# A four-layer graph network on one core: the order of its preparation, of its edge products and of the unread products on TensorE

## What is computed

```
x = layernorm(x + L0(x, adj))   # A_hat @ x, Linear(128, 256), batch norm, relu, Linear(256, 128), batch norm
x = layernorm(x + L1(x, adj))   # U^T @ x, Linear, relu, Linear, U @ out
x = layernorm(x + L2(x, adj))   # 4 attention heads over the 256 edges, softmax by source node
x = layernorm(x + L3(x, adj))   # two graph convolutions, then LSTMs of 1 to 4 steps over the nodes

# L1: the eigenvectors of the normalised Laplacian
deg = A.sum(0) + A.sum(1) - diag(A)
L_norm = deg**-.5 * (diag(deg) - A) * deg**-.5
_, U = eigh(L_norm)                         # 128 x 128, eigh reads the symmetric part
```

## Time and profile before

| | |
|---|---|
| three executions | 1038.46, 1037.54 and 1037.67 us, median 1037.67 |
| the profiled execution | 1037.68 us |
| its span | 1035.9 us, mean granted clock 0.921 |
| PE | 928.0 us busy (90%) |
| PEld | 606.9 us (59%) |
| DVE | 615.2 us (59%) |
| ACT | 603.3 us (58%) |
| POOL | 159.2 us (15%) |

### The profile page before, as it was taken

The page is one execution under the profiler, slowest core; times in us unless marked ns, Lnnn a source line. Parts: engine busy times, 40 slices in busy tenths (PEclk is TensorE's granted clock), DMA queues, the critical chain, the costliest instruction groups (busy, mean ns, idle before and its releaser), DMA issues.

```text
span 1035.9 us, 13392 instructions
## 1 busy us (share of the span) xinstructions
PE 928.0 (90%) x3987; PEld 606.9 (59%) x3987; DVE 615.2 (59%) x2155; ACT 603.3 (58%) x1520; POOL 159.2 (15%) x458
## 2 busy tenths in 40 slices
PE   3799867878888986999999999999999999999994
PEld 2555554455556664666888777885444466654442
DVE  5577766745668784477445797434544444544676
ACT  0456646736537773277644355535966688875556
POOL 0233333313333332000000000000000000000055
PEclk9799977867779896799999999999999999999998
DMA  9100000000000000000000000000000000000014
GB/s 257 49 1 1 0 1 1 1 1 1 1 1 2 1 1 1 1 1 1 1 1 1 1 2 1 1 1 0 1 1 0 1 0 1 1 0 1 0 41 122
DMA packets 14328, 12.99 MB, mean 13 GB/s; under 512 B 896, under 2 KB 11056, under 8 KB 14256
## 3 DMA queue, kind: packets, MB, share of 16 engines
q1 hardware_dynamic: 14018, 11.98, 4.1%
q10 hardware_dynamic: 238, 0.16, 0.1%
HBM read 7.89 MB, written 4.19 MB: 12 GB/s over the span
## 4 chain that ended last, share of the span: by engine, by line
PE 73%; DVE 16%; ACT 6%; issue 3%; DMA 1%; POOL 1%; ACTq 0%; DVEq 0%; POOLq 0%
PE bank L938 17%; PE bank L962 9%; PE bank L857 3%; PE bank L799 3%; PE bank L789 3%; PE bank L813 3%; PE bank L847 3%; PE bank L620 2%; PE bank L619 2%; PE bank L506 2%; PE bank L753 2%; PE bank L764 2%; PE bank L925 1%; PE bank L865 1%; PE bank L917 1%
## 5 line engine op out<-in xcount | busy, mean ns | idle before, releaser
L1409 ACT ACTIVATE hid_t<-bank,gate_b 128x512 f32<-128x512 f32 (+1 forms) x252 | 148.9, 630 | 48.9 <-PE bank L962 48.2
L1518 POOL TENSOR_SCALAR x<-x,perm 128x128 f32<-128x128 f32 x32 | 29.3, 928 | 592.7 <-DVE perm L2169 592.7
L962 PE MATMUL bank<-ms,w_t 128*128 128x512 f32 (+1 forms) x288 | 110.8, 528 | 0.1
L938 PE MATMUL bank<-hid_t,w_t 128*128 128x336 f32 (+1 forms) x296 | 106.6, 506 | 1.2 <-DVE x L2144 1.2
L938 PE MATMUL bank<-feat_t,w_t 128*128 128x512 f32 x208 | 93.1, 603 | 0.0
L938 PEld LDWEIGHTS bank<-hid_t,w_t 128*128 128x128 f32 x296 | 55.8, 190 | 46.2 <-issue 25.8
L962 PEld LDWEIGHTS bank<-ms,w_t 128*128 128x128 f32 x288 | 54.1, 190 | 48.1 <-issue 33.8
L938 PEld LDWEIGHTS bank<-feat_t,w_t 128*128 128x128 f32 x208 | 39.1, 189 | 51.0 <-issue 46.7
L1197 ACT ACTIVATE con<-bank,con 128x1 f32<-128x1 f32 x62 | 16.2, 261 | 89.3 <-PE bank L620 89.2
L1416 ACT ACTIVATE hid_t<-hid_t 128x512 f32<-128x512 f32 (+1 forms) x72 | 41.8, 581 | 34.9 <-DVE hid_t L2128 25.6
L1043 ACT ACTIVATE x<-x,perm 128x128 f32<-128x128 f32 x128 | 52.3, 482 | 2.6 <-DVE perm L1550 2.6
(11 more groups left out here) (420 smaller groups left out, 2121.7 us busy)
## 6 DMA issues: line engine op xcount, KB each, us to landing
out<-x SPq DMA_DIRECT2D x16, 256.0 KB, 3.0
con<-in_constants SPq DMA_DIRECT2D x1, 449.0 KB, 3.1
feat_t<-in_L_gnn_W SPq DMA_DIRECT2D x2, 128.0 KB, 3.6
e_int<-in_L_gnn_src ACTq DMA_DIRECT2D x1, 128.0 KB
l_w<-in_L_gnn_W SPq DMA_DIRECT2D x2, 64.0 KB
wg<-in_L_gnn_Wg SPq DMA_DIRECT2D x2, 64.0 KB
adj_n<-in_adj SPq DMA_DIRECT2D x1, 64.0 KB, 3.3
x<-in_x SPq DMA_DIRECT2D x4, 0.5 KB, 10.3
```

What stands on the lines that cost most here:

```text
L938: return mm(bank[4 * u + BANK_OF[g]][:, 0:w], w_t[:, WB_IH + 4 * (it.p - 1) + g, :], lstm_x(n), start=True, stop=(it.k == 0))
L962: mm(bank[4 * u + BANK_OF[g]][:, 0:w], w_t[:, WB_HH + 4 * (it.p - 1) + g, :], lstm_h_of(it.chain)[:, 0:w], start=False, stop=True).then_in ...
L1409: f(dst[:, 0:w], bank[4 * u + BANK_OF[g]][:, 0:w], ACT.Tanh if g == G_G else ACT.Sigmoid, bias=gate_b[:, 4 * (it.p - 1) + g:4 * (it.p - 1) ...
```

## The change

**Preparation.** DVE converts the edge numbers first, PE turns them and the first group of weights early. ACT makes the one-hot rows in place of DVE: 1 - |i - s| cut at zero by an Abs and a Relu of 128 columns for each half of the edges (`edge_columns`), the rank by a Sign of 256 columns that adds up its own row, then again Abs and Relu of 256 columns (`edge_places`). DVE keeps the key, two conversions and a doubled iota. DVE's `eigen_setup` follows right behind the Laplacian; `ahat_t`, the row sums and the columns of `v_rows` come behind it (`graph_columns`). The memsets stand at the start.

**Turn 0.** The edge products are spread over it: sources ahead of the first `pe_rows`, targets behind w, ends behind the diagonals, rows beside step 1, adjacency and starts behind step 1's rank update. DVE copies two of them (`edges_sorted`) behind its first next vector, ACT four (`edges_kept`, `edges_spread`) behind the row copy of step 2. The rest of DVE's edge work (`edge_rest`) stands at the start of layer 1.

**Layer 0.** All its constants are one slot higher. The first quarter of `x` has a semaphore of its own, on which the first aggregate waits; the fifth waits for the rest.

**Unread products.** `kept_busy` by slots is gone. In each turn but 0 and 8 stand two of 384 columns (`filled`): behind step 1's rank update, and ahead of the transposition. `without_products(slot)` is true for slots with no layer 0 work on PE (23, 40 to 44, 61 to 63), where `beside` adds 384 and 128 columns. Two of 384 stand ahead of `pe_kept_turned(HALF)` and one of 128 behind it.

**Order in a turn.** On PE, `beside(h2)` with layer 0's work stands ahead of the transposition, not behind it. DVE's next vector of step 1 stands ahead of the tangents, and ACT's part of it ahead of the row norm.

**Buffers.** `pair`, `pv_ident`, `kept` and `square` are new tiles of their own, in place of parts of `con`, `src_st`, `src_1h` and `dst_s`; the tangents use `con_f` and `con_b` in place of `perm`; the unread tiles `ys` go.

The core of the diff:

```diff
-QUIET, FULL_FROM = (41, 42, 43, 60, 61, 62), 36
-A_AGG, A_COPY, A_HID0, A_HID1, A_SAVE0, A_SAVE1, A_STATS = 0, 1, 1, 2, 2, 2, 4
-BN_ONE, B_RELU, B_OUT, B_KEEP, B_STATS = 20, 22, 23, 24, 25
+A_AGG, A_COPY, A_HID0, A_HID1, A_SAVE0, A_SAVE1, A_STATS = 1, 2, 2, 3, 3, 3, 5
+BN_ONE, B_RELU, B_OUT, B_KEEP, B_STATS = 21, 23, 24, 25, 26
...
             def beside(slot):            # PE
...
+                if without_products(slot):
+                    filled(384, slot == HALF - 1)
+                    filled(128, slot == HALF - 1)
...
+            def filled(cols, rows_read):
+                into = bank[5] if rows_read else bank[6]
+                mm(into[:, P:P + cols], ident, con[:, 0:cols], start=True, stop=True)
...
             def jacobi_turn(i):          # PE
...
-                pe_rows(h0)
-                kept_busy(h0)
-                pe_w(i)
-                beside(h0)
...
+                if i == 0:
+                    first_products(h0)
+                else:
+                    pe_rows(h0)
+                    pe_w(i)
+                    beside(h0)
...
                 behind_rank(h0)
                 pe_rows(h1)
-                kept_busy(h1)
+                if i == 0:
+                    edges_rows()
                 beside(h1)
                 pe_rank(h1)
                 behind_rank(h1)
+                if i == 0:
+                    edges_adjacent()
+                    edges_starts()
+                else:
+                    filled(384, True)
                 pe_rows(h2)
-                kept_busy(h2)
+                beside(h2)
+                filled(384, False)
                 pe_turn(i)
-                beside(h2)
                 pe_rank(h2)
...
+                filled(384, False)
+                filled(384, False)
                 pe_kept_turned(HALF, 1)
+                filled(128, False)
...
             def edge_places():           # ACT, new
+                for c in range(EC):
+                    link.mark(f(perm[:, c, :], sum_st[:, :], ACT.Sign, bias=rank[:, 0, c:c + 1], accum_out=rank[:, 1, c:c + 1]))
+                link.settle()
+                act.wait_ge(s["edge_cols"], 5)
+                for c in range(EC):
+                    link.mark(f(away[c][:, :], iota2, ACT.Abs, bias=rank[:, 1, c:c + 1]))
+                link.settle()
+                for c in range(EC):
+                    t = f(perm[:, c, :], away[c][:, :], ACT.Relu, scale=-0.5, bias=ones[:, 0:1])
+                t.then_inc(s["edge_hot"], 1)
...
             def jacobi_turn(i):          # ACT
...
                     act_matrix(h1)
-                act_row_norm(i)
                 if h1 is not None:
                     act_vector(h1 + 1)
+                act_row_norm(i)
                 behind_step(h1)
...
             def jacobi_turn(i):          # DVE
...
                 dve_reflected(h1)
+                dve_next(h1)
                 dve_tangents(i)
-                dve_next(h1)
```

269 lines of the change are left out of this document (150 added, 119 removed).

## The result

The changed kernel takes 999.26 us (median of 998.09 to 999.61), the kernel before 1038.07. The ratio is 0.9623 (95% interval 0.9607 to 0.9640): 38.8 us less. Run once more among the experiments it took 998.35 us (ratio 0.9617, 0.9601 to 0.9633). The forecast was 1009.0, in a range of 1000 to 1021. So the sign was right, the gain was 10 us larger than forecast, and the time lies 0.7 us under the range.

What follows compares the result with a forecast made beforehand. In the turns a chain of small steps over four engines was taken as the bound, if PE is on time. 1037.68 - 15.5 (preparation) - 2.0 (turn 0) - 12.0 (turns 1 to 15) + 0.8 (behind) gave 1009.0 us, range 1000 to 1021.

Steps and rivals of the forecast that it cites:

- turns 1 to 15: Unread products fill PE's gaps and hold the clock up: items of 15.1 us, taken as 12.0 less (5 to 18).
- the next vector ahead of the tangents: Second step of each turn: vector earlier but tangents as much later, taken as 0, 4 us either way in all.
- behind the turns: Ahead of the solve: two unread products before the turning of the kept columns delay PE, 0.8 us more.
- The preparation: Until DVE's first reflected row: it starts at about 15.4 instead of 30.90, 15.5 us less (13.5 to 16.5).
- Turn 0: First reflected row to turn 1: 22.3 us instead of 24.35, 2.0 less (5 less to 2 more).
- Turns 1 to 4: 22.4 us three times and 21.6, with 0.6 lost per turn to layer 0 ahead of the transposition: 0.8 less.
- Turn 5: ScalarE's 4.07 us wait for the batch norm's moments stays; 0.5 us less.
- The discount of 3.1: Turns 1 to 15: 12.0 us taken instead of 15.1, as some turns' new products and surrounding work would miss.
- That all gaps are filled: Rival: all gaps filled, also in the solve, with 3 us more in turn 0: 1001 us, chance 0.12.
- The start did not stall: Rival that the start stalls on ScalarE's one-hot chain and the late first kept column: 1013 us, chance 0.10.
- The slower rival: At 1.2 GHz, unread and layer 0 products cost some 3 us per turn on the chain: 1063 us, chance 0.02.
- the signs named: Reflected row at 15 to 16 us, turn 1 from 37 to 38, clock near 1.00 in turns 6, 7, 9 to 14.

Runs made afterwards that it cites:

- changed again: The changed kernel itself run once more, nothing altered, as the base for the runs beside it: 998.35 us, ratio 0.9617.
- before + new unread products: The kernel before with only the new unread products in the turns, its own ones gone, order and preparation as before: 1018.41 us, ratio 0.9809.
- the transposition ahead: The changed kernel with the transposition ahead of layer 0's products and the unread one in each turn's third step: 1024.20 us, ratio 0.9860.

## Why the prediction was right or wrong

The mechanism was right: the products in PE's gaps hold the clock up, and the start moves by what was forecast. Two terms of the sum were mis-sized. The 12.0 us for turns 1 to 15 measured 17.5 and 19.9 in the two traces, and the next vector ahead of the tangents, put at 0, is worth 3 to 4 of them. A third, behind the turns, had the wrong sign in the traces.

**The preparation: right.** L1770's successor (L1838) came at 15.59 us, forecast 15.4; 15.3 us less, forecast 15.5. The first edge product came at 12.01, forecast 12.4. ScalarE's operation of 256 columns took 0.51 us and not the 0.40 of the sum, which was read from a copy of that size, but the chain was early enough all the same. By the Trainium skill (ScalarE: Activation LUTs, What ACT_TABLE_LOAD costs) the estimate was 0.49, and the trace agrees with it.

**Turn 0: right, in part by luck.** From the first reflected row to turn 1 it was 22.4 us (15.59 to 37.99), forecast 22.3; in the second trace it was 20.6. The forecast had the clock up before step 1; it was in the second trace, and in the first it was down again (last section).

**Turns 1 to 4: the sum right, by two misses that cancel.** 0.7 us less, forecast 0.8. Turns 1 to 3 took 22.1 to 22.3 us each, forecast 22.4; turn 4 took 22.2, forecast 21.6, as the clock fell in it. Layer 0 ahead of the transposition costs 0.45, 0.46 and 0.26 us in turns 1 to 3 (forecast 0.6), by the kernel with layer 0 behind it at the same clock. Turn 5: 0.3 to 0.7 less, forecast 0.5. Its wait stands, and turn 11's too; ScalarE in turn 11 of the changed kernel:

```profile
265.01 0.20 ACT L1150 ACTIVATE sc<-sc 128x1 f32<-128x1 f32 x1 [4.38 <-DVE sc L1725]
```

**Turns 1 to 15: the sign right, the size the step that failed.** The items added up to 15.1 us, and 12.0 was taken, for turns in which the clock would fall all the same. Item by item:

| us less | forecast | changed | changed again | before + new unread products |
|---|---|---|---|---|
| turns 1 to 4 | 0.8 | 0.7 | 0.7 | 4.0 |
| turn 5 | 0.5 | 0.3 | 0.7 | 2.0 |
| turns 6 and 7 (to its last row product) | 2.4 | 3.8 | 3.8 | 2.4 |
| rest of 7, removal turn | 0 | -0.5 | -0.9 | -0.4 |
| turn 9 | 3.4 | 5.1 | 3.8 | 4.3 |
| turn 10 | 2.3 | 3.7 | 3.7 | 2.5 |
| turn 11 | 1.0 | 0.5 | 2.7 | 2.0 |
| turns 12 to 15 | 4.7 | 4.0 | 5.3 | 0.8 |
| together | 15.1 | 17.5 | 19.9 | 17.6 |

The discount of 3.1 was wrong: the clock still fell in turns 5, 8, 11 and 12 to 15, but turns 11 to 15 missed their items by no more than 1.2 us in one trace and passed them by 2.3 in the other, and in turns 6, 7, 9 and 10 it held nearly everywhere and they passed theirs. The items of turns 6, 7 and 10 were right for the unread products alone; what the changed kernel has above them there is the order. That the sum for turns 12 to 15 came near in the changed kernel and not with the products alone was not foreseen.

**The next vector ahead of the tangents: the step that failed by its mechanism.** It was taken at 0, because the tangents would come as much later. They do come later, but the transposition waits behind layer 0's and the unread product anyway, so nobody is late. It is worth 3 to 4 us by the run that undoes it, 0.6 in each of the turns 6 and 10 and 0.1 in turns 1 to 3. This lies inside the bounds of 4 us that the prediction gave, and the value between them was the wrong one.

**Behind the turns: the sign wrong in the traces, the size not told from nothing.** Forecast was 0.8 more. The traces show the solve 0.9 and 1.7 us shorter, with a part of it at full clock. What was to cost 0.8 cost about 0.2 by two traces: without the products PE waits 1.02 us for the kept column's load at that place, and the two fill it (from the start of turn 15's last product to the turning it is 1.41 us without them and 1.61 with them). Leaving the three out made no measurable difference in the median.

**Layers 1 to 3.** The 2.4 us less of the first trace belong to the clock at the start of layer 1, and the second trace has none of it.

**The sum.** The forecast was 28.7 us less (1037.68 - 1008.98). The spans of the two traces are 38.1 and 40.2 less, so 9.4 and 11.5 were missing. Of these, 5.5 and 7.9 are in turns 1 to 15 (3.1 for the discount, the rest about what the tangents' order brings), 1.7 and 2.5 behind the turns, 2.4 and -0.1 in layers 1 to 3, -0.3 and 1.9 in turn 0, and 0.1 and -0.7 ahead of the first row product. The last three move with the clock's chance and the start from trace to trace.

**The rivals.** That all gaps are filled (0.12, 1001 us) came nearest, though its gaps were not all filled: 72 and 55 us of turns 1 to 15 are still at the low clock, and the tangents' gain made up for it. The start did not stall: the first kept column was issued at 28.5 us, and DVE's fourth next vector, at 36.11 in the first trace, did not wait for it. The slower rival's mechanism is real, at another place: the run with work of 5 us between transposition and rank update at the low clock lost 26 us. Of the signs named, turn 1 from 37 to 38 us, the clock in turns 6 and 7 and the rank update 0.06 us behind its vector came as forecast; the clock was near 1.00 in turns 12 to 14 only in the second trace, and in turn 11 in neither (0.75 and 0.87).

## What to carry to other kernels

Where small steps bound a kernel and TensorE's clock falls in their gaps, put work that is ready, needed or not, ahead of the matmul that waits for another engine. All of it between that matmul and the next of the chain cost 26 us here, with the same instructions; a part of it there cost 3 to 4 us in all, and saved 0.3 to 0.45 in each of the turns 1 to 3. Price a stretch at the low clock by what stands in it: 0.15 to 0.2 us per us in a chain of small matmuls, 0.3 where large ones stand ahead of the chain. When two engines' work is reordered, ask who waits for each result in the new program, not in the old one.

## What the runs showed of the hardware

The records of the granted clock begin some time after the start (at 15.4 us in the first trace of the changed kernel, at 25.6 in that of the transposition ahead), and rows before that show 1.00 though matmuls run at half speed: the first edge product (4 records of 256 columns) took 2.07 us at 12.01. When the clock rises, and whether it falls again in turn 0, differs from run to run. The third edge product (`edges_ends`, L480), of the same size, took 2.05 us at 19.92 in one trace of the changed kernel and 1.11 in the other:

```profile
19.53 1.11 PE L480 MATMUL bank<-perm,dst_1h 128*128 128x256 f32 x4
```

So turn 0 took 24.0 and 21.8 us in two traces of the same kernel, and up to 25.2 in kernels whose turn 0 was the same. Later falls of the clock come or stay away in the same way (turn 11: 27.7 and 25.4 us), and yet the two medians of this kernel are 0.9 us apart.
